# Six-layer decoder on one core: another agents' stage, alternating steps on VectorE, gates without diagonals, and new step sequences

## The chip, the core and the metric

The kernel runs on one NeuronCore of a Trainium2 chip. Its engines run their own instruction streams and meet through semaphores: TensorE (PE for matmuls, PEld for the loading of their stationary operand), VectorE (DVE), ScalarE (ACT), GpSimd (POOL) and SyncE (SP), which here issues all transfers. The metric is the device time of one execution in microseconds (us). The kernel before took 1081.24 us, the median of three runs from 1078.39 to 1082.4.

## The reference, cut to what matters

32 batches of 100 tokens, 256 features, fp32. Six layers follow each other, each ending in x = layernorm(x + layer(x)):

```
L0_attn : agent = x @ wq.w_conv1 ; key vector, softmax over 256, softmax over tokens, weighted sum of v -> one row per batch
L0_xattn: cross attention on ctx (361 keys) with a mask, 1 head
L0_ffn  : top 50 of 100 tokens by a sigmoid gate, 16-head attention among them
L1_attn : banded 16-head attention over all 100 tokens
L1_xattn: cross attention on ctx, 1 head
L1_ffn  : x/rms quantised to int8 steps (127/absmax, round, clip), times an int8 weight, times a scale
```

The first layer needs little per token: for each batch one 256-vector, scaled by a per-token factor `tok`, is added to x. All of its 32 vectors are computed ahead of everything else; that part is called the agents' stage here. Its steps: agent = x.w; y = the sum over tokens of agent times x; key row = y @ w_k0, softmaxed over 256 features; z = w_v0 times it; logits = z.x per token, softmaxed over tokens; u = the sum over tokens of that weight times x; the agent's vector v = u @ w_v0T.

## The kernel before, in words

**Streams and turns.** Two batches make a pair. Four streams A, B, C, D work on one pair each; a turn is one pair through all six layers, and each stream has four turns, 16 jobs in all. Each stream has its own SBUF tiles and two PSUM banks. Each engine's program for a stream is a Python generator whose `yield`s cut it into segments. `ORDER` holds one string per engine; `take` runs one segment of the named stream per letter, so the order on every engine is fixed, and an engine whose next segment waits does nothing else meanwhile. The strings come from a planner that is not part of the file.

**The agents' stage** (`tensor_agents`, `scalar_agents`, `vector_agents`, `gpsimd_agents`, and the transfers in `sync_first`) runs ahead of the turns on every engine. Eight slots of four batches are loaded. PE transposes x (L320), ACT copies the transposes out (L638), DVE computes `ag` (L804). When all transposes are done PE forms y as rows (L327: `ag` broadcast to 32 columns as the stationary operand, x moving, 256 columns). ACT and DVE copy the rows out of PSUM (`row`, L633 and L813), and `rows_to_columns` (L307) turns them into columns: 16 matmuls whose stationary operand is a 128x128 block. L336 is the key row, L307 is used again behind L392 (the rows u), L400 gives the vectors. The softmax over tokens is eight exponentials with sums on ACT (L647), a reciprocal and a division on DVE (L858), and L385, which turns the weights into columns. Products of weights for later layers (L299, L374, L380 and others, copied by `product`) lie between these steps on PE and DVE. The finished vectors go from SBUF to a DRAM tensor `agent_rows` (L1275), and `load_agent` (L1225) reads each pair's 2 KB row back, repeated over 100 partitions.

**Entry to the turns.** GpSimd clears the lower rows of `work` (L1111) and then `v_pick` and `v` of all streams (L1117, L1118), and goes on to its turns. DVE and ACT wait for the first of these (`agent_pool("rows")`), PE for `agent_dve("v")`; all wait for `ld_const`, every remaining weight.

**Masks.** `cell` and `seq` are single buffers for all streams. For each job GpSimd multiplies them (L1158), DVE makes two passes (L891, L893), ACT takes the logarithm (L665), GpSimd adds (L1162); only then does SP load the masks of the next stream in turn (`job`). In the first turn each stream's DVE program starts with its masks.

**Layernorm.** `stats` (L876) per batch: the residual `r`, then `bn_stats` (L878), then `bn_aggr` (L880), each waiting for the one before it; then the same for the second batch of the pair. GpSimd raises the variance to the power -1/2 (L1126), and `normalize` (L885) scales both batches.

**Gates.** DVE computes the gate of each token, multiplies the identity by it (L966, two diagonals), PE multiplies a matrix of ones by the diagonals (L473) so that each partition holds all gates, and DVE ranks them (L974, L977, batch after batch) and builds a selection matrix (L981). PE transposes that (L478) and gathers the chosen tokens (L482).

**Quantised layer** (L1076 to L1098): five small steps in a row, two scalings of 256 columns (L1085), rounding and clipping on 512 columns (L1088, L1090), then transposes and the product.

Of the kernel before, what the change touches and what calls it, by code (L numbers as in the profile page):

```python
# [50 lines left out]
class Steps:  # L51
# [8 lines left out]
    def up(self, name):  # L60
# [5 lines left out]
NORM = "r0 bn0 ag0 r1 bn1 ag1 x0 x1"  # L66
# [3 lines left out]
    "pick": "gates selT gath q k v hs0 hs tr0 tr1 av fo sc0 sc1",  # L70
# [7 lines left out]
    "pick": "ez selT xT q vs0 ex0 ex1 eT0 rT fo",  # L78
# [8 lines left out]
    "pick": "z0 z1 gp gt dg0 dg1 tie0 rk0 tie1 rk1 pk0 pk1 kT vs1 mx0 mx1 rd eT1 aT " + NORM,  # L87
    "local": "k0 k1 v1 " + " ".join(f"ma{i} mb{i} rd{i} eT{i} aT{i}" for i in range(NB * NC)) + " " + NORM,
    "second": "mx0 nb0 mx1 nb1 pT0 rs aT1 " + NORM,
    "quant": "am am2 am3 ra sc y0 y1 up yq os " + NORM,  # L90
}
GPSIMD = {
    "mask": "prod sum",
# [9 lines left out]
AGENT_TENSOR = ("w " + " ".join(f"x{n}" for n in range(16)) + " " + " ".join(f"y{n}" for n in range(8))  # L103
                + " yT1 key p0 p1 arT z p2 p3 log p4 p5 p6 col " + " ".join(f"u{n}" for n in range(8)) + " yT2 vec")
AGENT_SCALAR = " ".join(f"x{n}" for n in range(16)) + " row1 toke kexp lexp row2"
AGENT_VECTOR = ("w " + " ".join(f"ag{n}" for n in range(8)) + " tokd row1 tokr tok yT1 kmax p0 p1 krec kn aT zT p2 p3 lmax "
                "p4 p5 p6 lrec ln acol row2 w8 yT2 v")
# [10 lines left out]
def program(nc, ins, out):  # L118
    ctx = ExitStack()
    with ctx:  # L120
# [11 lines left out]
        qscale = sb("qscale", [P, 1])  # L132
# [18 lines left out]
        tok = sb("tok", [S, B])  # L151

# [3 lines left out]
        class Stream:  # L156
            def __init__(s, n):
# [22 lines left out]
                s.diag = s.eT[0:S, 0:T].rearrange("p (b t) -> p b t", b=NB)  # L180
                s.tie, s.above = s.eT[0:S, T:T + S], s.eT[0:S, T + S:T + 2 * S]
                s.pick = s.eT[0:S, T + 2 * S:T + 2 * S + NB * P].rearrange("p (b m) -> p b m", b=NB)
# [32 lines left out]
                s.ra = sb(f"ra{n}", [S, NB])  # L215
                s.os = sb(f"os{n}", [S, NB])
                s.load_x = Loaded(sem(f"load_x{n}"), 1)
                s.load_agent = Loaded(sem(f"load_agent{n}"), 1)
# [29 lines left out]
        y_rooms = [s.v[:, :, :, :].rearrange("p b h m -> p (b h m)")[:, 0:2 * D].rearrange("p (i d) -> p i d", i=2) for s in streams]  # L248
# [7 lines left out]
        b_room = SB_.kT[:, :, :, :].rearrange("p j c t -> p (j c t)")  # L256
        ag, tokd, toke, tokr, acol = (b_room[0:S, k * B:(k + 1) * B] for k in range(5))
        yT, aT_a, zT = (b_room[:, k * B:(k + NC) * B].rearrange("p (c b) -> p c b", c=NC) for k in (5, 7, 9))
        lstat = b_room[:, 11 * B:11 * B + 3 * SLOTS].rearrange("p (k i) -> p k i", k=3)
        a_room = SC_.kT[:, :, :, :].rearrange("p j c t -> p (j c t)")  # L260
        agent_w, arow, arow2 = a_room[:, 0:D], a_room[0:B, D:2 * D], a_room[0:B, 2 * D:3 * D]
        agent_v = SD.aT[0:B, :, :].rearrange("p c t -> p (c t)")[:, 0:D]
        astat = sb("astat", [B, 4])
# [9 lines left out]
        agent_rows = nc.dram_tensor("agent_rows", (NPAIR, NB * D), F32).ap()  # L273
        agent_kept = sem("agent_kept")
        ld_w0, ld_wk, ld_c, ld_const = (sem(n) for n in ("ld_w0", "ld_wk", "ld_c", "ld_const"))
# [4 lines left out]
        agent_pool = Steps(sem("agent_pool"), "rows zeros")  # L280
# [15 lines left out]
        def tensor_agents(e):  # L296
# [6 lines left out]
            def rows_to_columns():  # L303
                for c in range(NC):
                    for i in range(SLOTS):
                        at_ = (c * SLOTS + i) * ROWS
                        last = e.matmul(psum[:, 7, at_:at_ + ROWS], y_rooms[i // 2][:, i % 2, c * P:(c + 1) * P],  # L307
                                        ident[:, 0:P:32], start=True, stop=True)
                return last
# [13 lines left out]
            for i in range(SLOTS):  # L323
# [15 lines left out]
            e.wait_ge(ld_c, LD_C)  # L339
            spread(4, cols["a_bv"], W["a_o"]).then_inc(*agent_pe.up("p0"))  # L340
            spread(5, cols["c_bk"], W["c_qT"]).then_inc(*agent_pe.up("p1"))
# [10 lines left out]
            spread(4, cols["c_bv"], W["c_o"]).then_inc(*agent_pe.up("p2"))  # L352
            for c in range(NC):
                last = e.matmul(psum[:, 5, 0:1], cols["c_bk"][:, c:c + 1].to_broadcast([P, P]), cols["c_bq"][:, c:c + 1],
                                start=c == 0, stop=c == NC - 1)
            last.then_inc(*agent_pe.up("p3"))
# [9 lines left out]
            e.wait_ge(*agent_dve("p3"))  # L366
# [4 lines left out]
            last.then_inc(*agent_pe.up("p4"))  # L371
            for h in range(NC):
# [10 lines left out]
            e.wait_ge(*agent_dve("ln"))  # L383
            for i in range(SLOTS):
                last = e.matmul(psum[0:S, 7, i * ROWS:(i + 1) * ROWS], l_rooms[i // 4][:, i % 4, :], ident[:, 0:P:32],  # L385
                                start=True, stop=True)
            last.then_inc(*agent_pe.up("col"))
            e.wait_ge(*agent_dve("acol"))
            for i in range(SLOTS):
                for j in range(ROWS):  # L390
                    b = ROWS * i + j
                    last = e.matmul(psum[32 * j:32 * j + 32, i // 2, i % 2 * D:(i % 2 + 1) * D],  # L392
                                    acol[:, b:b + 1].to_broadcast([S, 32]), x_of(b), start=True, stop=True)
                last.then_inc(*agent_pe.up(f"u{i}"))
            e.wait_ge(*agent_act("row2"))
            e.wait_ge(*agent_dve("row2"))
            rows_to_columns().then_inc(*agent_pe.up("yT2"))
            e.wait_ge(*agent_dve("yT2"))
            for c in range(NC):
                last = e.matmul(psum[0:B, 6, 0:D], yT[:, c, :], W["w_v0T"][:, c, :], start=c == 0, stop=c == NC - 1)  # L400
            last.then_inc(*agent_pe.up("vec"))
            e.wait_ge(*agent_dve("v"))
            e.wait_ge(ld_const, LD_CONST)
# [249 lines left out]
        def scalar_turns(e, s):  # L653
# [42 lines left out]
            for t in range(TURNS):  # L696
# [20 lines left out]
                if t == 0:  # L717
                    e.wait_ge(*agent_pool("zeros"))
# [749 lines left out]
```

## Time and profile before

| what | value |
|---|---|
| median of 3 runs | 1081.24 us |
| the profiled execution, its own time | 1081.67 us |
| span of its profile | 1079.9 us |
| PE busy | 900.4 us, 83% |
| DVE busy | 704.7 us, 65% |
| ACT busy | 514.2 us, 48% |
| POOL busy | 371.4 us, 34% |
| mean granted TensorE clock | 0.876 |

Times in the profile count from the start of the span. Busy time is the time in which an engine has at least one instruction; a granted clock of 1.00 is TensorE's 2.4 GHz and 0.50 is 1.2 GHz. The profiled execution ran 0.43 us above the median.

### The profile page before, as it was taken

How to read it: one execution, taken by the hardware profiler on the slowest of the kernel's cores; microseconds unless marked ns; L12 is line 12 of the kernel's file. 1: busy time of each engine (PE TensorE's matmuls, PEld its weight loads, DVE VectorE, ACT ScalarE, POOL GpSimd, SP SyncE). 2: the span in 40 equal slices, each digit the busy share in tenths (PEclk: the TensorE clock that was granted, in tenths of full speed). 3: DMA queues.
4: the chain of work that ended last, by engine and by line, in shares of the span. 5: the costliest groups of instructions: out<-in, count | busy, mean ns of one | idle time of the engine just before them, and what ended most of it. 6: DMA issues, size and time to landing. Idle time of an engine off the chain costs nothing.

```text
span 1079.9 us, 19738 instructions
## 1 busy us (share of the span) xinstructions
PE 900.4 (83%) x7022; PEld 671.0 (62%) x7022; DVE 704.7 (65%) x2081; ACT 514.2 (48%) x2392; POOL 371.4 (34%) x528
## 2 busy tenths in 40 slices
PE   7957798898798699998889788897979688997983
PEld 5735677565577587665567566574647466765662
DVE  4235666565777857567697876558487686766576
ACT  3102244766542345865433355664535144556641
POOL 0045401344463322254443422236144232223243
PEclk9766898999888799997889699898869898998896
DMA  7801400002214000002032200011030400000000
GB/s 227 285 32 44 157 1 2 2 8 85 92 55 144 24 1 2 2 23 73 30 123 75 78 9 2 12 69 34 11 102 1 144 17 1 1 2 1 1 1 31
DMA packets 23382, 54.10 MB, mean 50 GB/s; under 512 B 3696, under 2 KB 9588, under 8 KB 23284
## 3 DMA queue, kind: packets, MB, share of 16 engines
q1 hardware_dynamic: 23284, 52.84, 14.7%
q8 instruction: 55, 0.90, 0.3%
q14 instruction: 43, 0.35, 0.1%
HBM read 49.53 MB, written 3.31 MB: 49 GB/s over the span
## 4 chain that ended last, share of the span: by engine, by line
PE 50%; DVE 26%; ACT 10%; POOL 5%; issue 4%; DMA 4%; SPq 1%; DVEq 0%; POOLq 0%; ACTq 0%
PE psum L419 8%; PE psum L424 8%; PE psum L458 7%; ACT work L763 4%; PE psum L444 4%; DVE bn L878 4%; PE psum L578 4%; PE psum L589 3%; ACT work L728 3%; DVE x L885 3%; PE psum L599 2%; DVE mx L1040 2%; PE psum L581 2%; DVE res L945 1%; DVE mv L880 1%
## 5 line engine op out<-in xcount | busy, mean ns | idle before, releaser
L763 ACT ACTIVATE work<-psum,mx 100x100 f32<-100x100 f32 x512 | 169.8, 369 | 53.1 <-DVE mx L1040 52.8
L1124 POOL TENSOR_SCALAR ve<-mv 100x2 f32<-100x2 f32 x96 | 21.7, 226 | 289.7 <-DVE mv L880 289.4
L763 ACT ACTIVATION_READ_ACCUMULATOR work<-psum,mx 100x1 f32 x512 | 118.5, 232 | 0.0
L657 ACT ACTIVATE xT<-psum 128x100 f32<-128x100 f32 (+3 forms) x144 | 53.0, 374 | 124.5 <-PE psum L594 55.9
L458 PE MATMUL psum<-eT,ctx 128*128 128x100 f32 x768 | 103.6, 292 | 7.0 <-DVE eT L914 6.7
L458 PEld LDWEIGHTS psum<-eT,ctx 128*128 128x128 f32 x768 | 99.6, 207 | 10.5 <-DVE eT L914 8.9
L1153 POOL COPY work<-rden 100x128 f32<-100x128 f32 (+1 forms) x80 | 25.1, 314 | 201.4 <-DVE rden L1044 172.6
L444 PE MATMUL psum<-ctxT,qT 128*100 128x361 f32 x256 | 92.6, 508 | 2.1 <-ACT qT L657 1.2
L657 ACT ACTIVATE eT<-psum 100x400 f32<-100x400 f32 (+3 forms) x128 | 64.1, 513 | 49.1 <-PE psum L617 21.2
L878 DVE BATCH_NORM_STATS2 bn<-res 100x6 f32<-100x256 f32 x192 | 82.1, 427 | 6.6
L1040 DVE TENSOR_REDUCE mx<-psum 100x4 f32<-100x400 f32 x128 | 66.9, 565 | 26.4 <-PE psum L581 26.2
L589 PE MATMUL psum<-ident,work 100*100 100x100 f32 x512 | 71.8, 273 | 14.1 <-ACT work L763 13.8
L885 DVE TENSOR_SCALAR x<-res,mv,rstd 100x256 f32<-100x256 f32 x160 | 73.5, 504 | 13.4 <-POOL rstd L1126 13.0
L728 ACT ACTIVATE work<-psum,mx 128x50 f32<-128x50 f32 x256 | 73.8, 349 | 16.4 <-DVE mx L999 16.3
L589 PEld LDWEIGHTS psum<-ident,work 100*100 100x100 f32 x512 | 54.5, 140 | 30.3 <-ACT work L763 22.8
L1126 POOL TENSOR_TENSOR rstd<-ve,minus_half 100x2 f32<-100x2 f32 x96 | 69.3, 722 | 8.0
L578 PE MATMUL psum<-kT,qT 64*100 64x400 f32 x256 | 64.5, 583 | 6.7 <-DVE aT L1051 6.6
L444 PEld LDWEIGHTS psum<-ctxT,qT 128*100 128x100 f32 x256 | 44.4, 181 | 36.0 <-issue 8.0
L1146 POOL TENSOR_TENSOR kT<-work,heads 128x400 f32<-128x400 f32 x64 | 54.4, 853 | 32.9 <-DVE work L1029 32.9
L728 ACT ACTIVATION_READ_ACCUMULATOR work<-psum,mx 128x1 f32 x256 | 63.3, 253 | 0.0
L1046 DVE COPY eT<-psum 100x400 f32<-100x400 f32 x64 | 35.5, 554 | 38.1 <-PE psum L589 37.8
L414 PE MATMUL psum<-ident,x 100*128 100x100 f32 x192 | 31.9, 294 | 28.7 <-DVE x L885 28.6
(231 smaller groups left out, 2066.3 us busy)
## 6 DMA issues: line engine op xcount, KB each, us to landing
ctx<-in_ctx SPq DMA_DIRECT2D x16, 768.0 KB, 7.0
ctxT<-in_ctxT SPq DMA_DIRECT2D x16, 722.0 KB, 4.3
cell<-in_cell SPq DMA_DIRECT2D x16, 282.0 KB
seq<-in_seq SPq DMA_DIRECT2D x16, 282.0 KB
x<-in_x SPq DMA_DIRECT2D x16, 200.0 KB
eT<-agent_rows SPq DMA_DIRECT2D x16, 200.0 KB
out<-xplus SPq DMA_DIRECT2D x16, 200.0 KB
work<-in_x SPq DMA_DIRECT2D x4, 400.0 KB
```

The lines of the kernel that those rows point to most:

```text
L419: last = e.matmul(dst, w[:, c, h * P:(h + 1) * P], n(c), start=c == 0, stop=c == NC - 1)
L424: last = e.matmul(dst, xT(c), w[:, c, :], start=c == 0, stop=c == NC - 1)
L444: last = e.matmul(bk[b][0:S, 0:S2], s.qT[:, c, b * S:(b + 1) * S], s.ctxT[:, b, c, :], start=c == 0, stop=c == NC - 1)
L458: last = e.matmul(bk[b][:, c * S:(c + 1) * S], s.ctx[:, b, j, c * P:(c + 1) * P], s.pT[:, b, j, :], start=j == 0, stop=j == S2C - 1)
L578: e.matmul(bk[g][0:S, 0:4 * S], s.qT[r:r + 64, c, b * S:(b + 1) * S], s.keys[r:r + 64, i % 2, :, :], start=True, stop=False, skip_group_ch ...
L589: last = e.transpose(bk[g][0:S, q * S:(q + 1) * S], s.e[:, 4 * g + q, :], ident[0:S, 0:S])
L657: return e.activation(dst, src, ACT.Copy, **kw)
L728: last = e.activation(s.e_pick[:, 4 * g + i, j, 0:CAP], bk[g][:, at_:at_ + CAP], ACT.Exp, bias=s.mx[:, h:h + 1], accum_out=s.den[:, h:h + 1])
L763: last = e.activation(s.e[:, h, :], bk[g][0:S, q * S:(q + 1) * S], ACT.Exp, bias=s.mx[0:S, h:h + 1], accum_out=s.den[0:S, h:h + 1])
L878: e.bn_stats(s.bn[:, b, :], s.res[0:S, b, :]).then_inc(*dve.up(f"bn{b}"))
L885: e.tensor_scalar(dst[0:S, b, :], s.res[0:S, b, :], s.mv[:, b, 0:1], s.rstd[:, b:b + 1], ALU.subtract, ALU.mult).then_inc(*dve.up(f"x{b}"))
L1040: e.tensor_reduce(s.mx[0:S, 4 * g:4 * g + 4], bk[g][0:S, 0:4 * S].rearrange("p (h k) -> p h k", k=S), AX, ALU.max, negate=True).then_inc(* ...
```

## The change

**Agents' stage.** y is formed as columns at once: per batch and half of the features one matmul with x (100x128) as the stationary operand and one column of `ag` moving. Each slot's eight such matmuls stand behind the transposes of the next slot. The softmax over tokens subtracts the maximum on DVE (two instructions), takes two exponentials without sums, and is not divided; its sum comes from one matmul with ones and scales the finished vector. The vectors stay in SBUF (`agent_v`, 32 partitions); each is copied from its one partition to the 100 partitions of a stream's tile by a transfer of its own. The weight products p1, p3, p4, p5, p6 stand later on PE.

**Masks and transfers.** In the first turn each stream has its own room for the masks. All four are loaded early and go through the agents' programs of POOL, DVE and ACT; the turns start with the mix. PE and the others wait for the first few weights (`ld_first`) at the entry and for the rest at the first pick. `zeros` moves into the turns of POOL.

**Turns.** The steps of both batches alternate (r0 r1 bn0 bn1 ag0 ag1), as do those of the ranking; the diagonals go; the gather precedes the transposes of the selection; the quantised layer loses two small steps and rounds batch by batch. All five sequences in `ORDER` are new (PE 816 letters as before, DVE 748 for 752, ACT 716 for 720, POOL 364 for 368, SP 52 for 58); their letters are left out here.

```diff
-NORM = "r0 bn0 ag0 r1 bn1 ag1 x0 x1"
+NORM = "r0 r1 bn0 bn1 ag0 ag1 x0 x1"
# tensor_agents
+            def weighed(i, weights):
+                for j in range(ROWS):
+                    b = ROWS * i + j
+                    for c in range(NC):
+                        last = e.matmul(psum[:, 7, c * B + b:c * B + b + 1], x_of(b)[:, c * P:(c + 1) * P],
+                                        weights[:, b:b + 1], start=True, stop=True)
+                return last
...
-            for i in range(SLOTS):
-                e.wait_ge(*agent_dve(f"ag{i}"))
-                for j in range(ROWS):
-                    b = ROWS * i + j
-                    last = e.matmul(psum[32 * j:32 * j + 32, i // 2, i % 2 * D:(i % 2 + 1) * D],
-                                    ag[:, b:b + 1].to_broadcast([S, 32]), x_of(b), start=True, stop=True)
-                last.then_inc(*agent_pe.up(f"y{i}"))
-            e.wait_ge(*agent_act("row1"))
-            e.wait_ge(*agent_dve("row1"))
-            rows_to_columns().then_inc(*agent_pe.up("yT1"))
+                if i:
+                    e.wait_ge(*agent_dve(f"ag{i - 1}"))
+                    weighed(i - 1, ag).then_inc(*agent_pe.up(f"y{i - 1}"))
+            e.wait_ge(*agent_dve("ag7"))
+            weighed(SLOTS - 1, ag).then_inc(*agent_pe.up("y7"))
...
# vector_agents, behind the logits
+            for k in range(2):
+                e.tensor_tensor(l_rooms[k], psum[:, k, :].rearrange("p (i t) -> p i t", t=P)[:, :, 0:S],
+                                lstat[:, 4 * k:4 * k + 4].unsqueeze(2).to_broadcast([P, SLOTS // 2, S]), ALU.add).then_inc(
+                    *agent_dve.up(f"sub{k}"))
...
+            for s in streams[2:4]:
+                masks_clip(e, s, 0)
+            e.wait_ge(*agent_pe("vec"))
+            e.tensor_scalar(agent_v[:, :], psum[0:B, 6, 0:D], astat[:, 3:4], None, ALU.mult).then_inc(*agent_dve.up("v"))
...
# gpsimd_agents
+            for s in streams:
+                masks_product(e, s, 0)
+            for s in streams:
+                masks_sum(e, s, 0)
+            e.wait_ge(*SD.gpsimd["mask"]("sum", 0))
             e.wait_ge(*agent_pe("u7"))
             for s in streams:
                 last = e.memset(s.work[32 * (ROWS - 1):P, 0:H * HALF], 0.0)
             last.then_inc(*agent_pool.up("rows"))
...
# vector_turns
-            def stats(dve, t, b):
-                e.wait_ge(*dve(f"r{b}", t))
-                e.bn_stats(s.bn[:, b, :], s.res[0:S, b, :]).then_inc(*dve.up(f"bn{b}"))
-                e.wait_ge(*dve(f"bn{b}", t))
-                e.bn_aggr(s.mv[:, b, :], s.bn[:, b, :]).then_inc(*dve.up(f"ag{b}"))
+            def stats(dve, t):
+                for b in range(NB):
+                    e.wait_ge(*dve(f"r{b}", t))
+                    e.bn_stats(s.bn[:, b, :], s.res[0:S, b, :]).then_inc(*dve.up(f"bn{b}"))
+                for b in range(NB):
+                    e.wait_ge(*dve(f"bn{b}", t))
+                    e.bn_aggr(s.mv[:, b, :], s.bn[:, b, :]).then_inc(*dve.up(f"ag{b}"))
...
# load_agent, and the place of it in sync_first
         def load_agent(e, s, t):
-            e.dma_start(s.agent.rearrange("p b d -> p (b d)"),
-                        agent_rows[s.pair(t):s.pair(t) + 1, :].to_broadcast([S, NB * D])).then_inc(s.load_agent.sem, 16)
+            for b in range(NB):
+                n = NB * s.pair(t) + b
+                e.dma_start(s.agent[:, b, :], agent_v[n:n + 1, :].unsqueeze(1).to_broadcast([1, S, D])).then_inc(s.load_agent.sem, 16)
...
             e.wait_ge(*agent_dve("v"))
-            e.dma_start(agent_rows.rearrange("n (b d) -> (n b) d", b=NB), agent_v).then_inc(agent_kept, 16)
-            e.wait_ge(agent_kept, 16)
             for s in streams:
                 load_agent(e, s, 0)
+            for s in (SC_, SD):
+                load_ctx(e, s, 0)
```

DVE's new sequence begins `BADCABDCABAC`: the mixes of B, A, D and C stand ahead of the first `normalize`, which is A's. `weighed` multiplies in fp32, as all matmuls here do except the quantised layer's and the band's.

## Rows read from the trace of the kernel before

**Rows 1.** The page's busy time of each engine, and the chain of waits by engine.
```profile
PE 900.4 (83%) x7022; PEld 671.0 (62%) x7022; DVE 704.7 (65%) x2081; ACT 514.2 (48%) x2392; POOL 371.4 (34%) x528
PE 50%; DVE 26%; ACT 10%; POOL 5%; issue 4%; DMA 4%; SPq 1%; DVEq 0%; POOLq 0%; ACTq 0%
```

**Rows 2.** Windows: stretch, length, busy time and instructions per engine, clock, DMA share, GB/s.
```profile
83.00:160.00 77.00, 64.37 (x430) 51.55 (x430) 45.95 (x144) 25.70 (x96) 26.34 (x27) 0.83 0.20 70
160.00:1000.00 840.00, 720.79 (x5734) 535.71 (x5738) 576.92 (x1680) 439.94 (x2110) 303.64 (x436) 0.89 0.12 39
1000.00:1080.00 80.00, 56.75 (x404) 39.79 (x396) 53.78 (x152) 32.62 (x146) 27.20 (x45) 0.82 0.03 11
```

**Rows 3.** Timeline of PE to the first turn: start, length, line, tiles, forms, count.
```profile
4.80 2.07 PE L299 MATMUL psum<-res,w_conv_c 128*128 128x256 f32 x4 [4.80 <-DMA ident<-in_ident]
20.71 1.59 PE L320 MATMUL psum<-ident,ctxT 100*128 100x100 f32 x8 [1.10 <-DMA ctxT<-in_x]
29.41 5.54 PE L307 MATMUL psum<-ident,v 128*128 128x4 f32 x32 [0.92 <-DVE v L813]
43.38 1.11 PE L299 MATMUL psum<-xplus,c_bv_c 128*128 128x256 f32 x4
48.97 0.34 PE L362 MATMUL psum<-aT,kT 128*32 128x100 f32 x8
55.84 1.58 PE L385 MATMUL psum<-ident,qT 128*100 128x4 f32 x16 [1.99 <-DVE qT L858]
57.70 3.14 PE L392 MATMUL psum<-work,kT 100*32 100x256 f32 x32 [0.28 <-DVE kT L862]
70.19 1.92 PE L400 MATMUL psum<-xplus,kT 128*32 128x256 f32 x4 [0.32 <-DVE kT L869]
83.06 0.90 PE L414 MATMUL psum<-ident,x 100*128 100x100 f32 x4 [10.96 <-DVE x L885]
```

**Rows 4.** Windows of line L307 on PE alone: stretch, length, busy, clock, DMA.
```profile
29.00:31.00 2.00, 1.59 (x15) 0.99 1.10 308
31.00:35.00 4.00, 3.95 (x19) 0.50 1.06 353
```

**Rows 5.** Timeline of DVE: the agents' stage, and the first mixes.
```profile
7.72 0.42 DVE L804 SCALAR_TENSOR_TENSOR x<-work,kT 100x256 f32<-100x256 f32 x1
8.07 0.42 DVE L804 SCALAR_TENSOR_TENSOR x<-work,kT 100x256 f32<-100x256 f32 x1
72.15 0.41 DVE L871 COPY aT<-psum 32x256 f32<-32x256 f32 x1 [2.01 <-PE psum L400]
78.40 0.48 DVE L945 SCALAR_TENSOR_TENSOR res<-eT,tok,x 100x256 f32<-100x256 f32 x1
78.91 0.43 DVE L878 BATCH_NORM_STATS2 bn<-res 100x6 f32<-100x256 f32 x1
79.47 0.45 DVE L945 SCALAR_TENSOR_TENSOR res<-eT,tok,x 100x256 f32<-100x256 f32 x1
80.42 0.18 DVE L880 BATCH_NORM_AGGREGATE mv<-bn 100x2 f32<-100x6 f32 x1
119.56 0.45 DVE L966 TENSOR_SCALAR eT<-ident,gate 100x100 f32<-100x100 f32 x2
120.95 0.48 DVE L945 SCALAR_TENSOR_TENSOR res<-eT,tok,x 100x256 f32<-100x256 f32 x1
```

**Rows 6.** Timeline of POOL: the clearing of four tiles, and one mask sum.
```profile
63.14 3.90 POOL L1111 MEMSET work<- 32x1024 f32 x4 [62.70 <-PE psum L392]
79.49 2.01 POOL L1162 TENSOR_TENSOR kT<-cell,kT 100x722 f32<-100x722 f32 x1 [2.22 <-ACT cell L665]
```

**Rows 7.** Two windows of all engines, as in rows 2, and one transfer issue.
```profile
75.00:79.00 4.00, 0.00 (x0) 0.00 (x0) 1.55 (x4) 0.40 (x1) 2.23 (x2) 0.50 0.57 194
261.00:263.00 2.00, 2.00 (x10) 1.56 (x11) 1.93 (x6) 1.94 (x13) 0.16 (x1) 1.00 1.02 406
agent_rows<-aT SPq DMA_DIRECT2D x1, 32.0 KB, 1.4
```

More of the change, by code:

```diff
@@ L351, in tensor_agents @@
             last.then_inc(*agent_pe.up("z"))
[L352 to L356, printed above, removed]
+            spread(5, cols["c_bv"], W["c_o"]).then_inc(*agent_pe.up("p2"))
             e.wait_ge(*agent_dve("zT"))
@@ L371, in tensor_agents @@
             last.then_inc(*agent_pe.up("p4"))
+            e.wait_ge(*agent_act("row2"))
+            e.wait_ge(*agent_dve("row2"))
+            for c in range(NC):
+                for i in range(SLOTS):
+                    at_ = (c * SLOTS + i) * ROWS
+                    last = e.matmul(psum[:, 7, at_:at_ + ROWS], u_rooms[i // 2][:, i % 2, c * P:(c + 1) * P],
+                                    ident[:, 0:P:32], start=True, stop=True)
+            last.then_inc(*agent_pe.up("yT2"))
+            e.wait_ge(*agent_dve("yT2"))
+            for c in range(NC):
+                last = e.matmul(psum[0:B, 6, 0:D], yT[:, c, :], W["w_v0T"][:, c, :], start=c == 0, stop=c == NC - 1)
+            last.then_inc(*agent_pe.up("vec"))
+            e.wait_ge(*agent_dve("p3"))
             for h in range(NC):
@@ L382, in tensor_agents @@
             last.then_inc(*agent_pe.up("p6"))
[L383 to L403, printed above, removed]
+            e.wait_ge(ld_first, LD_FIRST)
         def tensor_turns(e, s):
@@ L623, in tensor_turns, with masks_log @@
                 yield
+        def masks_log(e, s, t):
+            part = mask_rooms(s, t)[0]
+            e.wait_ge(*s.vector["mask"]("clip", t))
+            e.activation(part, part, ACT.Ln).then_inc(*s.scalar["mask"].up("ln"))
         def scalar_agents(e):
             e.preload_act_table_set("natural_log_exp_and_others")
-            def row(name, first, last_, scale):
-                for k, after in ((0, first), (1, last_)):
-                    e.wait_ge(*agent_pe(after))
-                    last = e.activation(y_rooms[k].rearrange("p i d -> p (i d)"), psum[:, k, :], ACT.Copy, scale=scale)
-                last.then_inc(*agent_act.up(name))
             for n in range(NC * SLOTS):
@@ L773, in scalar_turns @@
                 if t + 1 < TURNS:
-                    masks(t + 1)
+                    masks_log(e, s, t + 1)
                     yield
@@ new lines, in vector_agents @@
+            product(wqbk[:, :], 4, 1)
+            product(bqbk[:, :], 5, 3)
+            e.wait_ge(*agent_pe("col"))
+            e.tensor_copy(acol, psum[0:S, 7, 0:B]).then_inc(*agent_dve.up("acol"))
+            e.wait_ge(*agent_pe("sum"))
+            e.reciprocal(astat[:, 3:4], psum[0:B, 6, D:D + 1]).then_inc(*agent_dve.up("rsum"))
+            for k, ready in ((2, "u5"), (3, "u7")):
+                e.wait_ge(*agent_pe(ready))
+                last = e.tensor_copy(u_rooms[k][:, :, :].rearrange("p i d -> p (i d)"), psum[:, k, :])
@@ L1103, in vector_turns, with masks_product, masks_sum @@
                 yield
-        def gpsimd_agents(e):
+        def masks_product(e, s, t):
+            part, other = mask_rooms(s, t)
+            e.wait_ge(*s.load_mask(t))
+            e.tensor_tensor(part, part, other, ALU.mult).then_inc(*s.gpsimd["mask"].up("prod"))
+        def masks_sum(e, s, t):
+            e.wait_ge(*s.scalar["mask"]("ln", t))
+            e.tensor_tensor(s.lm[:, :, :], mask_rooms(s, t)[0], s.lm[:, :, :], ALU.add).then_inc(*s.gpsimd["mask"].up("sum"))
+        def gpsimd_agents(e):
+            for s in streams:
+                masks_product(e, s, 0)
+            for s in streams:
+                masks_sum(e, s, 0)
+            e.wait_ge(*SD.gpsimd["mask"]("sum", 0))
             e.wait_ge(*agent_pe("u7"))
@@ L1112, in gpsimd_agents @@
             last.then_inc(*agent_pool.up("rows"))
[L1113 to L1119 removed]
+            e.wait_ge(ld_first, LD_FIRST)
         def gpsimd_turns(e, s):
```

419 lines of the change are left out of this document (202 added, 217 removed).

## The prediction

> **What bounds the kernel now.** I read the busy times first, then the chain, then windows from end to end, then the agents' stage and the first mixes on each timeline. PE is busy 83% of the span, yet half of the chain of waits runs over other engines, DVE with 26% ahead of them [rows 1]. So neither PE's work alone nor one engine's latency sets the time; four streams keep PE filled up to a point. I measure PE's work as busy time times granted clock. In the long middle it is 720.79 x 0.89 / 840 = 0.764 us per us [rows 2]. From 83 to 160 us 64.37 x 0.83 = 53.4 us get done, which the middle's pace would do in 69.9 us; the ramp therefore loses 7.1 us. That is less than its look suggests (the fourth stream's mix is at 120.95 us [rows 5], 42.6 us behind the first), because two or three streams nearly fill PE. The first 83 us hold no turn at all: PE's first transposes for a turn are at 83.06 [rows 3].
>
> **The clock at the start.** The records give no lower clock before 31 us, but the matmuls do: the four of L299 take 2.07 us at 4.80 and 1.11 us at 43.38 [rows 3]. So the first stretch runs at 1.2 GHz, transposes and all. L307 shows the two levels in one block: 15 records in 1.59 us at 0.99, 19 in 3.95 us at 0.50 [rows 4], or 0.11 and 0.21 us a record, with two records to a matmul, and that while PE was busy without a gap.
>
> **Part 1, y as columns.** Out go L327, the row copies and the first L307, which ends at 29.41 + 5.54 = 34.95 us [rows 3]. In come 64 matmuls, 128 records, that load a stationary operand as wide as L307's for one moving column; no row shows this form, and L307's 0.21 us is the nearest. The stage then is one block on PE: it starts at 6.87 (L299's end), eight slots of transposes at 1.59 make 12.7 us, 128 x 0.21 make 26.9, and the end is at 46.5 us, 11.5 later than now. At the other level it would be 14.1 us for the sums and 33.7 us for the end, 1.3 earlier; both are kept as ends. I take the slow one: neither the transposes, at 80% of PE's time, nor L307, at all of it, held or won the full clock in this trace, and the new block is nothing but these two kinds. The arrival of x (the last slot at 20.71) no longer matters.
>
> **Part 2, from there to the vectors.** Now 34.95 to 72.56 (L871's end [rows 5]) is 37.6 us. The logits end at 49.31 and their columns start at 55.84 [rows 3]; in between are a maximum, eight exponentials, a reciprocal and a division. The new order has a maximum, two additions and two exponentials half beside each other: 3.0 us for 6.5, a gain of 3.5. One weight product of 2 us (L299's form) leaves the way ahead of the transposed key row: gain 2. Moved in are p4 between u and its columns (1 us) and the sum's matmul (0.3). Mask passes of C and D now stand in front of the vectors' copy on DVE; PE's 1.92 us of L400 [rows 3] covers most of them, and I add 0.1. Gain 4.1; bounds 0 and 7. The vectors are ready at 46.5 + 33.5 = 80.0 us for 72.56.
>
> **Part 3, the copies of the vectors.** Eight transfers of 100 KB each read one SBUF partition a hundred times. Nothing like it is in the trace. Today's four transfers from DRAM move 800 KB inside the 4 us window from 75 us [rows 7]: the low end, all eight there 5 us behind the vectors. The only transfer that reads this tile takes 1.4 us for its 32 KB [rows 7], 23 GB/s: the high end, 35 us. Between them lies the pace of a single queue engine: 406 GB/s on 16 of them [rows 7] is 25.4 each. If one partition gives its bytes to one engine's worth of traffic at a time, a copy takes 102.4 KB / 25.4 = 4.0 us and eight take 32. I take this, nearest to the row that reads the same tile.
>
> The Trainium skill, "SBUF — State Buffer", section "Door 1: The DMA port swizzle", speaks against the change here too: a transfer's bandwidth depends on how many of 16 ports its partitions reach, and one partition reaches one. With its 436 GB/s over 16 ports a copy would be 3.8 us and the eight 30 us (an estimate from the page); the forecast would be 2 us lower. No row here reads from one partition.
>
> The wait is placed badly. DVE's sequence has the mixes of B, A, D and C ahead of the first normalisation, so all four streams stand behind the last copy. D's mix starts at 80.0 + 1 for the latency + 32 = 113. DVE then has two mixes of 1.73 (below), POOL's root meanwhile, and a normalisation of 0.7: PE's first transposes come at 117.2 for 83.06, 34.1 later. What would stand there if the copies were fast is POOL: at the vectors two mask sums of 2.01 and the clearing of 3.90 [rows 6] are left, so DVE may enter at 88; four mixes and a normalisation give 95.7 on PE, 12.6 later than now.
>
> **Part 4, the ramp.** All masks are done, so four streams start together. I let the new ramp lose 3 us (some 4 to 6 us at half clock) for 7.1: gain 4.1, bounds 0 and 7.
>
> **Part 5, the turns.** A mix of two batches takes 80.42 + 0.18 - 78.40 = 2.20 us [rows 5]: a step that waits for the one before starts 0.51 us behind it (78.40 to 78.91), an independent one 0.35 (7.72 to 8.07). Alternating, r0 r1 bn0 bn1 ag0 ag1 end at 1.73, a gain of 0.47. It counts fully in mix, pick, local and quant, 64 times, 30 us; in the two cross stages the first batch's steps now wait for the second's result, and I count 0.2 for 32 of them, 6 us. The diagonals are 0.45 us each pair [rows 5], 16 times, 7 us; ranking, quantising and the gather ahead of the transposes together 1 us a job, 16 us. PE's share of the gates stays as it is (two 100-column matmuls for one of 200). Sum 59 us of steps, not all on the path: DVE has 26% of a 1079.9 us chain for 704.7 busy, 0.40 [rows 1], so 24 us by that. Since a shortened step often uncovers another wait I take 14; bounds 0 and 24. The sequences themselves are worth plus or minus 8.
>
> The Trainium skill, "VectorE: DVE Perf Modes", section "The DRAIN you can't avoid", says that waits between VectorE's instructions cost nothing and only their number counts. By that rule alternation is worth nothing. The 0.51 and 0.35 above disagree with it, so I give it a small chance below.
>
> Later turns also load their vectors this way, 24 copies of 4.0 us instead of 12 transfers. They are issued well ahead, but x of the next turn queues behind them: cost 4, bounds 0 and 20.
>
> **Sum.** 34.1 - 4.1 - 14 + 4 = +20.0 us on the profiled execution's own 1081.67 (span 1079.9 and 1.8 around it; 0.43 above the median): 1101.7, said as 1102 us. Chance 0.45, its own range 1088 to 1116.
>
> **Rivals.**
> - A, cheap copies: the eight vectors arrive within 5 us, and POOL's chain sets the start. 12.6 - 4.1 - 14 = -5.5: 1076 us, the side of faster. For it: four such transfers take 4 us today; against it: these read DRAM, not one partition. It decides wherever the eight copies need under about 10 us, since POOL covers that much. Chance 0.27.
> - B, full clock in the first block: y ends at 33.7, 12.8 earlier: 1089 us. For it: PE would be without gaps; against: so it was in L307. Chance 0.11.
> - A and B together: vectors at 67, POOL lets DVE in at 75, PE starts at 83: 1081.67 - 0.3 - 4.1 - 14 = 1063 us. Chance 0.09.
> - C, alternation saves nothing: 9 of the 14 us stay: 1111 us. Chance 0.08.
>
> **How the numbers follow.** About 0.5%, 5.4 us, is what a measurement of this kernel can tell from no change, so same is 1075.8 to 1086.7. A straddles its lower edge, half of it faster; A with B is faster; the forecast, B and C are mostly slower. Faster 0.12 + 0.09 + 0.08 from the low ends of the forecast and B (a larger part 5) = 0.29; same 0.13 from A and 0.05 from the edges of B and the forecast = 0.18; slower 0.53. The range takes in A with a few us below it and C with a few above, and leaves out most of A with B: 1066 to 1116.
>
> **What would show it.** Part 1: on PE's timeline the one-column matmuls at 0.21 us a record and the last near 46 us; under 36 us it was B. Part 3: the idle time of DVE's first `res` behind a transfer, the mix of D at 110 us or later; under 95 us it was A, and then POOL's clearing must end just before. Part 4: PE's windows behind its first turn should reach 0.76 at once. Part 5: starts of r0 and r1 0.35 apart, `bn` 0.35 apart, and a middle stretch whose pace is 1 to 2% above 0.764. If the middle is slower than now, the new sequences cost more than the steps give, which nothing in this trace can tell, and the sum is wrong there.

## The result, and the profile after

The changed kernel takes 1087.53 us, the median of 20 runs (1078.17 to 1097.23), beside 1081.01 us for the kernel before on the same chip: a ratio of 1.0058, with a 95% interval of 1.0037 to 1.0079. It is slower by 6.5 us. The forecast was 1102 us, 20 slower: the direction held and the range held it, the size did not. The profiled execution of the changed kernel took 1083.32 us, 4 below its median. The medians further down are of 4 to 10 executions; one of e4_ports's ten took 1626 us, and without it that median would be 1076.8 for 1077.2.

Page of the changed kernel, busy times and chain of waits, beside [rows 1]:
```profile
PE 888.7 (82%) x7088; PEld 678.3 (63%) x7088; DVE 660.4 (61%) x2062; ACT 511.2 (47%) x2376; POOL 377.4 (35%) x528
PE 54%; DVE 20%; ACT 10%; DMA 5%; SPq 4%; issue 3%; POOL 3%; DVEq 0%; POOLq 0%
```
DVE lost 44 us of work and a quarter of its share of the chain; DMA and SP's queue took 4 points more between them. Windows, as in [rows 2]:
```profile
83.00:160.00 77.00, 43.10 (x250) 35.30 (x251) 37.87 (x128) 15.13 (x51) 24.00 (x32) 0.77 0.26 56
160.00:1000.00 840.00, 717.71 (x5946) 541.63 (x5944) 541.10 (x1678) 447.78 (x2153) 307.24 (x437) 0.91 0.14 39
1000.00:1080.00 80.00, 59.08 (x402) 41.47 (x398) 53.79 (x156) 32.78 (x145) 28.09 (x44) 0.82 0.03 10
110.00:160.00 50.00, 42.82 (x250) 34.98 (x249) 30.30 (x102) 15.13 (x51) 21.43 (x27) 0.91 0.08 31
```
The first stretch does 43.10 x 0.77 = 33 us of work for 53 before, since no turn runs in it before 109.71. The middle runs at 717.71 x 0.91 / 840 = 0.778 for 0.764, and what is left over at the end is much the same. Once the turns have started, the pace is that of the middle at once: 42.82 x 0.91 / 50 = 0.779. PE's timeline, beside [rows 3]:
```profile
20.41 3.46 PE L311 MATMUL psum<-qT,work 100*128 100x1 f32 x16
39.16 6.87 PE L311 MATMUL psum<-qT,ctxT 100*128 100x1 f32 x32
48.19 2.08 PE L302 MATMUL psum<-a_o,a_bv_c 128*128 128x256 f32 x4
51.81 1.11 PE L302 MATMUL psum<-xplus,c_bv_c 128*128 128x256 f32 x4
109.71 1.57 PE L422 MATMUL psum<-ident,x 100*128 100x100 f32 x8 [32.60 <-DVE x L902]
```
The one-column matmuls take 3.46 / 16 = 0.216 us a record (0.21 forecast), and the block ends at 46.03; 46.5 was forecast. PE's first transposes for a turn come at 109.71 (83.06 before, 117.2 forecast): 26.7 us later than before, where the forecast had 34.1. Its 32.60 us of idle time end on DVE. DVE's timeline, and below it SP's:
```profile
74.30 0.47 DVE L883 TENSOR_SCALAR agent_v<-psum,vs 32x256 f32<-32x256 f32 x1
92.13 0.88 DVE L954 SCALAR_TENSOR_TENSOR res<-eT,tok,x 100x256 f32<-100x256 f32 x2 [14.28 <-DMA eT<-agent_v]
92.92 0.75 DVE L894 BATCH_NORM_STATS2 bn<-res 100x6 f32<-100x256 f32 x2
93.59 0.30 DVE L897 BATCH_NORM_AGGREGATE mv<-bn 100x2 f32<-100x6 f32 x2
93.81 0.86 DVE L954 SCALAR_TENSOR_TENSOR res<-eT,tok,x 100x256 f32<-100x256 f32 x2
105.85 0.88 DVE L954 SCALAR_TENSOR_TENSOR res<-eT,tok,x 100x256 f32<-100x256 f32 x2 [10.30 <-DMA eT<-agent_v]
```
```profile
74.80 22.79 SPq L1242 DMA_DIRECT2D eT<-agent_v  x8
```
The vectors are ready at 74.77 (80.0 forecast), B's mix stands behind the fourth copy at 92.13, D's behind the eighth at 105.85: 31.1 us for eight copies, 3.9 each, the forecast's 32 + 1. A mix of two batches takes 93.59 + 0.30 - 92.13 = 1.76 us from its first start to its last end (1.73 forecast), for 2.20 in [rows 5]. SP's queue itself is held 22.79 us over issuing the eight.

### The profile page after: what moved, and what is told of

Read it like the earlier page. It is cut to its first block, busy times and chain, and to the rows that moved or that the text cites. A ratio compares the mean times of both kernels' runs of the same rounds, so it can differ in the third digit from the quotient of the medians.

```text
span 1081.5 us, 19882 instructions
## 1 busy us (share of the span) xinstructions
PE 888.7 (82%) x7088; PEld 678.3 (63%) x7088; DVE 660.4 (61%) x2062; ACT 511.2 (47%) x2376; POOL 377.4 (35%) x528
## 4 chain that ended last, share of the span: by engine, by line
PE 54%; DVE 20%; ACT 10%; DMA 5%; SPq 4%; issue 3%; POOL 3%; DVEq 0%; POOLq 0%
PE psum L427 9%; PE psum L466 8%; PE psum L432 7%; ACT work L736 4%; PE psum L452 4%; ACT work L771 4%; PE psum L592 4%; PE psum L603 3%; DVE x L902 3%; DVE bn L894 3%; PE psum L311 2%; SPq L1242 2%; PE psum L613 2%; DMA x<-in_x 2%; DMA seq<-in_seq 2%
## 5 line engine op out<-in xcount | busy, mean ns | idle before, releaser
L771 ACT ACTIVATION_READ_ACCUMULATOR work<-psum,mx 100x1 f32 x512 | 122.5, 241 | 0.0
L902 DVE TENSOR_SCALAR x<-res,mv,rstd 100x256 f32<-100x256 f32 x160 | 78.7, 538 | 12.6 <-POOL rstd L1142 12.3
L452 PE MATMUL psum<-ctxT,qT 128*100 128x361 f32 x256 | 83.7, 470 | 1.6 <-ACT qT L687 1.4
L1142 POOL TENSOR_TENSOR rstd<-ve,minus_half 100x2 f32<-100x2 f32 x96 | 71.9, 749 | 8.0
L422 PE MATMUL psum<-ident,x 100*128 100x100 f32 x192 | 32.7, 292 | 51.0 <-DVE x L902 50.7
L894 DVE BATCH_NORM_STATS2 bn<-res 100x6 f32<-100x256 f32 x192 | 71.2, 412 | 0.0
L1162 POOL TENSOR_TENSOR kT<-work,heads 128x400 f32<-128x400 f32 x64 | 54.4, 860 | 28.1 <-DVE work L1035 28.1
L422 PEld LDWEIGHTS psum<-ident,x 100*128 100x128 f32 x192 | 22.9, 160 | 61.4 <-issue 34.2
```

Source lines behind the costliest of these rows:

```text
L452: last = e.matmul(bk[b][0:S, 0:S2], s.qT[:, c, b * S:(b + 1) * S], s.ctxT[:, b, c, :], start=c == 0, stop=c == NC - 1)
L771: last = e.activation(s.e[:, h, :], bk[g][0:S, q * S:(q + 1) * S], ACT.Exp, bias=s.mx[0:S, h:h + 1], accum_out=s.den[0:S, h:h + 1])
L894: e.bn_stats(s.bn[:, b, :], s.res[0:S, b, :]).then_inc(*dve.up(f"bn{b}"))
L902: e.tensor_scalar(dst[0:S, b, :], s.res[0:S, b, :], s.mv[:, b, 0:1], s.rstd[:, b:b + 1], ALU.subtract, ALU.mult).then_inc(*dve.up(f"x{b}"))
L1142: e.tensor_tensor(s.rstd[:, :], s.vare[:, :], minus_half[0:S, 0:NB], ALU.pow).then_inc(*pool.up("rstd"))
```

## The experiments

All times are medians; the kernel before had 1081.0 to 1082.8 us beside them, and each ratio is to it.

**1. Vectors through DRAM (e1_dram).**
```
+ e.dma_start(agent_rows..., agent_v[:, :]).then_inc(agent_kept, 16)
+ e.wait_ge(agent_kept, 16)
- for b in range(NB): e.dma_start(s.agent[:, b, :], agent_v[n:n + 1, :]...to_broadcast([1, S, D]))
+ e.dma_start(s.agent, agent_rows[pair:pair + 1, :].to_broadcast([S, NB * D]))
```


> The changed kernel, except that the agents' vectors go to the first mixes through DRAM as in the kernel before: one store of 8 rows, one wait, then one load of 200 KB per stream, instead of eight copies of 100 KB from one partition each. Theory S (the forecast's third part: the eight copies are what holds the start): the vectors are ready at 74.8 us as before the edit, the loads land some 6 us later (72.15 to 78.40 in the kernel before), VectorE enters the turns at 81.4 behind the zeroing on GpSimd, four mixes of 1.7 us, TensorE's first transposes at 88 to 89 us (109.7 now), the total 21 us shorter than the changed kernel: about 1067. Rival H (the copies only hide other work that is as late: masks, memsets, context loads): the first transposes stay behind 100 us and the total stays within 8 us of 1087.5. Rival M (the earlier start is given back, because the first turns then compete with the loads of the contexts C and D): the transposes start at 88 but the stretch up to 200 us loses over 8 us of it, total 1075 or more.

Measured: 1046.66 us, ratio 0.9665 (0.961 to 0.972). That is 41 us under the changed kernel, where theory S had 21. DVE and PE:
```profile
70.42 0.47 DVE L885 TENSOR_SCALAR agent_v<-psum,vs 32x256 f32<-32x256 f32 x1
77.57 0.88 DVE L956 SCALAR_TENSOR_TENSOR res<-eT,tok,x 100x256 f32<-100x256 f32 x2 [3.66 <-POOL work L1135]
84.75 1.56 PE L424 MATMUL psum<-ident,x 100*128 100x100 f32 x8 [11.57 <-DVE x L904]
```
From the vectors to the first transposes it is 84.75 - 70.89 = 13.9 us, for 109.71 - 74.77 = 34.9: 21 us, as S had it (the vectors themselves were ready 3.9 us earlier, of which more in the last section). The other 16 to 20 us came later in the kernel. DVE's waits in the changed kernel, in total, times and longest, show a candidate:
```profile
DVE res L954 <- DMA eT<-agent_v: 24.6, 2, 14.3
DVE res L954 <- DMA x<-in_x: 18.8, 2, 13.9
```
In the kernel before the second is 6.7 us in all, in the DRAM kernel 7.9. SP's and DVE's timeline of the changed kernel at that place:
```profile
863.91 1.53 SPq L1242 DMA_DIRECT2D eT<-agent_v  x2
865.55 0.43 SPq L1237 DMA_DIRECT2D x<-in_x  x1
875.47 0.88 DVE L954 SCALAR_TENSOR_TENSOR res<-eT,tok,x 100x256 f32<-100x256 f32 x2 [13.94 <-DMA x<-in_x]
```
The load of x goes out right behind a pair of copies (another pair went out at 855.13) and lands 10 us later.

**2. Only the later turns copy from one partition (e9_later_copies).**
```
+ source = agent_v[n:n + 1, :]...to_broadcast([1, S, D]) if t else agent_rows[n // NB, b * D:(b + 1) * D]...
```


> The changed kernel with the eight vectors of the first turn loaded from DRAM (100 KB each) and the 24 of the later turns copied from one partition each, as in the changed kernel. The kernel with all of them from DRAM took 1046.7 us, 41 less than the changed kernel, and its start was only 25 us earlier. Theory L (the later copies hold up what the same queue issues behind them: in the changed kernel VectorE waited 4.8 and 13.9 us for two loads of x issued right behind such copies): start at 85 us as with DRAM, the two waits for x back, total 1062 to 1067. Rival F (later copies cost nothing; the other 16 us came from the context loads C and D being issued late in the first turn, 97.6 to 104.9 us, or from another interleaving): total within 4 us of 1046.7, no wait for x over 5 us.

Measured: 1059.38 us (0.9759 to 0.985 as a ratio). It is theory L's case, a little under its 1062 to 1067: the later copies cost 12.7 us. Start and wait are as it says:
```profile
89.75 1.56 PE L424 MATMUL psum<-ident,x 100*128 100x100 f32 x8 [10.40 <-DVE x L904]
DVE res L956 <- DMA x<-in_x: 19.0, 2, 13.9
```
The waits for x have 11 us more than in the DRAM kernel (19.0 for 7.9), the total 12.7. So the eight first copies cost 1087.5 - 1059.4 = 28.1 us by the medians, 21.7 by the profiled spans (1081.5 and 1059.8). By the way from the vectors to PE's first transposes it is 21.1 (34.9 for 89.75 - 75.89 = 13.9).

**3. The copies in another order (e4_ports).**
```
+ for n in (0, 4, 1, 5, 2, 6, 3, 7): e.dma_start(streams[n // NB].agent[:, n % NB, :], agent_v[n:n + 1, :]...)
```


> The changed kernel with the same eight copies in another order: streams A and C in turn, then B and D, so that two copies that follow one another read partitions four apart (0, 4, 1, 5, ...). Theory Q (the copies of one queue are served one behind the other, each bound by its one partition, 3.9 us): the last one lands as late as now, near 105.5 us, and TensorE starts within 1 us of 109.7 (the stream whose turn is first may wait longer, at most 8 us more at the start). Rival P (neighbouring partitions share a path and could overlap if they were apart): the eight land in 16 to 20 us, near 93, and TensorE starts near 98, total about 1076.

Measured: 1077.19 us, ratio 0.9929 (0.9894 to 0.9965). Q falls, P holds:
```profile
78.15 14.06 SPq L1298 DMA_DIRECT2D eT<-agent_v  x8
95.39 0.88 DVE L954 SCALAR_TENSOR_TENSOR res<-eT,tok,x 100x256 f32<-100x256 f32 x2 [13.08 <-DMA eT<-agent_v]
102.05 1.35 DVE L902 TENSOR_SCALAR x<-res,mv,rstd 100x256 f32<-100x256 f32 x4
```
The vectors were ready at 78.12, DVE waited once, until 95.39, and then ran its four mixes without a gap: the eight land in 17.3 us for 31. The transfers' own pace says the same (windows of the changed kernel, then of this one; the last number is GB/s):
```profile
84.00:88.00 4.00, 0.00 (x0) 0.00 (x0) 0.00 (x0) 0.00 (x0) 0.00 (x0) 0.50 0.47 27
```
```profile
84.00:88.00 4.00, 0.00 (x0) 0.00 (x0) 0.00 (x0) 0.00 (x0) 0.69 (x1) 0.70 0.49 56
```

**4. The control for it (e11_tiles).** The same edit with (0, 2, 1, 3, 4, 6, 5, 7).

> The changed kernel with the eight copies in the order of partitions 0, 2, 1, 3, 4, 6, 5, 7: neighbours in the queue go to different streams' tiles, as in the run with the order 0, 4, 1, 5, ..., but read partitions of the same four. That run landed all eight in 17 us (31 in the changed kernel). Theory G (copies from partitions of the same group of four can't overlap, copies from different groups do): the first four serial, then the next four, first mixes behind D's copy at 30 to 31 us after the vectors, total as the changed kernel, 1085 to 1088. Rival W (what can't overlap is two copies into one tile): all landed 17 us behind the vectors, first transposes near 103, total near 1077.

Measured: 1083.85 us (1.0 to 1.0048). Vectors at 76.43, the last group's mix at 107.50, 31.1 us behind them:
```profile
107.50 0.88 DVE L954 SCALAR_TENSOR_TENSOR res<-eT,tok,x 100x256 f32<-100x256 f32 x2 [10.32 <-DMA eT<-agent_v]
```
The copies alternate between two tiles but stay within four partitions, and they don't overlap: it is the source partitions that count (theory G).

**5. The sums as rows (e2_yrows), 6. and with DRAM (e3_both).**
```
- weighed(i, ag)                      # 64 one-column matmuls into psum 7
+ matmul(psum rows, ag[:, b]...to_broadcast([S, 32]), x_of(b))   # 32, then two row copies each on ACT and DVE
+ rows_to_columns()                   # 16 matmuls of 4 columns
```


> The changed kernel, except that the weighted sums over the tokens are built as in the kernel before: as rows in PSUM, copied by ScalarE and VectorE, and turned into columns by 16 matmuls; the eight copies from one partition stay. Theory C (the 128 one-column matmuls cost 11.5 us at the start): the block ends near 35 us (46.0 now), the vectors are ready near 63.7 us if the stretch behind it keeps its 28.7 us, near 69 if TensorE's clock in it is the half one as in the kernel before; eight copies of 3.9 us behind them, the first transposes at 98.6 to 104, the total 1076 to 1082. Rival (the block is hidden, what follows waits for the weights' or x's loads): the vectors stay at 73 to 75 us, the total within 2 us of 1087.5.

> The changed kernel with both edits: sums as rows, vectors through DRAM. If the two prices stand behind one another (the forecast's way of adding them): vectors at 63.7 to 69 us, VectorE in the turns at 70.5 to 76, TensorE's first transposes at 78 to 83, the total 1056 to 1061, faster than both kernels. If the zeroing and the mask sums on GpSimd are the bound once both are gone: VectorE enters the turns at 81 whatever the vectors do, first transposes at 88, total 1067 as with the DRAM edit alone. If the turns' part of the change gives back what the start gains: about 1075 or more.

Measured: 1074.08 us (0.9917 to 0.9968), 13.4 under the changed kernel; and 1039.14 us (0.9528 to 0.9655), 7.5 under the DRAM kernel. PE and DVE with rows and copies (e2):
```profile
34.72 0.99 PE L311 MATMUL psum<-ident,a_v 128*128 128x4 f32 x4
68.43 0.47 DVE L895 TENSOR_SCALAR agent_v<-psum,vs 32x256 f32<-32x256 f32 x1
103.96 1.56 PE L427 MATMUL psum<-ident,x 100*128 100x100 f32 x8 [30.27 <-DVE x L914]
```
The block ends at 35.7 us for 46.0, so the columns cost 10.3 us on PE. From there to the vectors it is 33.2 us, for 28.7 in the changed kernel, and in the other two kernels with rows 32.4 and 32.0, for 28.6 to 32.7 in the other kernels with columns and the masks in the agents' stage (mean of these eight 30.1). So some 2 us of the 10 come back behind the columns, on average, and the single execution varies by more. The two prices stand behind one another: the rows take 13.4 us off the changed kernel, 7.5 off the DRAM kernel, and 7.9 in the pair of experiments 10 and 12.

**7. Alternation undone (e5_serial), 8. and done alone (e7_before_alt).**
```
- NORM = "r0 r1 bn0 bn1 ag0 ag1 x0 x1"     (e7: + in the kernel before, - in e5)
+ NORM = "r0 bn0 ag0 r1 bn1 ag1 x0 x1"
```


> The kernel with the vectors through DRAM (1046.7 us) and the residual steps of both batches one behind the other again, as before the change (r0 bn0 ag0 r1 bn1 ag1); everything else, the sequences too, stays. Theory A (the forecast's price: the alternation saves 9 us): 1056. Theory A2 (of the 45 us that the turns lost against the kernel before, alternation is the greater part, since these steps stand in the chain of waits): 1065 to 1075. Rival C (alternation saves nothing, the steps lie beside other work): within 3 us of 1046.7.

> The kernel before with one edit: the residual steps of both batches in turn (r0 r1 bn0 bn1 ag0 ag1), everything else as before, its sequences too. The reverse edit in a later kernel cost 20.5 us. Theory A2 (the alternation is worth 20 us by itself, since these steps stand in the chain of waits wherever they are): 1058 to 1063. Theory A (9 us, as forecast): 1070 to 1073. Rival I (the 20 us came from the fit between alternation and the rest of the change): 1076 to 1081.

Measured: 1067.17 us (0.9834 to 0.9963), 20.5 above its base; and 1061.19 us, ratio 0.9809 (0.9749 to 0.987), 19.8 under the kernel before. A2 both times. The mixes of e5:
```profile
81.92 0.48 DVE L954 SCALAR_TENSOR_TENSOR res<-eT,tok,x 100x256 f32<-100x256 f32 x1 [1.33 <-POOL work L1133]
83.00 0.45 DVE L954 SCALAR_TENSOR_TENSOR res<-eT,tok,x 100x256 f32<-100x256 f32 x1
84.05 0.47 DVE L954 SCALAR_TENSOR_TENSOR res<-eT,tok,x 100x256 f32<-100x256 f32 x1
```
From one pair's start to the next it is 84.05 - 81.92 = 2.13 us, for 1.68 in the changed kernel (92.13 to 93.81). Over the kernel DVE's busy time differs by 685.3 - 659.0 = 26.3 us in the first comparison and 704.7 - 673.2 = 31.5 in the second: 78 and 63% of it come out of the total.

**9. Diagonals and the longer quantised layer back (e12_long_quant).**
```
+ for b in range(NB): e.tensor_scalar(s.diag[:, b, :], ident[0:S, 0:S], s.gate[:, b:b + 1], None, ALU.mult)
+ e.tensor_scalar(s.sc, s.ra, 127.0, ...); "up" and "yq" over both batches at once
```


> The kernel with the vectors through DRAM (1046.7 us) and, as in the kernel before, the diagonals for the gates (two steps on VectorE, one matmul of ones with them) and the longer quantised layer (four single-column steps, rounding steps over both batches at once); alternation and sequences stay as changed. Theory 1 (5 us, as forecast): 1050 to 1054. Theory 2 (worth as much above the forecast as the alternation was, 2.3 times): 1056 to 1060. Rival (these steps lie beside other work): within 2 us of 1046.7.

Measured: 1055.04 us (0.9693 to 0.979), 8.4 above its base, between the two theories. DVE's busy time is 17.8 us more (676.8 for 659.0): 47% of it counts. With the 26.3 of the alternation these are 44.1 of the 44.3 us that DVE lost. The other steps of part 5, the ranking and the gather ahead of the transposes, were not tried by themselves.

**10. The sequences of the kernel before (e6_old_order).**
```
- "DVE": ("BADCABDCABACABABDBDCB...
+ "DVE": ("AABAABAACABABCABABADC...        # likewise PE, ACT, POOL, SP
```


> The kernel with the vectors through DRAM (1046.7 us) and the step sequences of the kernel before, fitted to the new numbers of steps (the mask steps of the first turn dropped, the zeroing step put in). Theory O (the sequences are worth 8 us at most either way, as forecast): 1039 to 1055. Theory O2 (the new sequences carry most of the 45 us that the turns gained): 1065 to 1085.

Measured: 1042.77 us (0.9606 to 0.9681), 3.9 under its base: the new sequences seem to cost a little. Four executions on each side (1038 to 1045 and 1038 to 1051) hardly bear such a difference; experiments 6 and 12 have 4.2 the same way. PE:
```profile
85.61 0.90 PE L424 MATMUL psum<-ident,x 100*128 100x100 f32 x4 [6.75 <-DVE x L904]
```
That is 10.2 us behind the vectors (75.38) for 13.9: the old order has A's mix and normalisation ahead of C's and D's mixes.

**11. The first turn's masks back in the turn (e13_masks_in_turns).**
```
+ if t == 0: masks_clip(e, s, 0); yield        # likewise product, log and sum; out of the agents' stage
```


> The kernel with the vectors through DRAM and the sequences of the kernel before (1042.8 us), with the first turn's mask steps (product, clip, logarithm, sum) moved from the agents' stage back into the first turn, as steps of the streams, as in the kernel before; the masks' tiles and their early loads stay. Theory 4 (the forecast: their place in the turn cost the ramp 4 us): 1045 to 1049. Theory R (what the other runs leave over of the difference between the kernels, 8 to 14 us, is this): 1051 to 1057. Rival N (beside other work in either place, and GpSimd's zeroing comes earlier without them): 1039 to 1044.

Measured: 1046.21 us (0.9623 to 0.9736), 3.4 above its base. It agrees with theory 4, but 3.4 us is no more than medians of four runs (1038 to 1045 and 1042 to 1053) can bear.

**12. The best of them (e10_best): DRAM, rows, old sequences.**

> The changed kernel with three edits: vectors through DRAM, sums as rows, and the step sequences of the kernel before. Alone, the first gave 1046.7, with the second 1039.1; the third took 3.9 us off the first. If they add: 1035 us, some 46 under the kernel before. If the old sequences only suited the start with the sums as columns: 1039 or above.

Measured: 1034.90 us, ratio 0.9564 (0.9518 to 0.9609): 46 us under the kernel before and 53 under the changed one. They add. Windows, as in [rows 2]:
```profile
83.00:160.00 77.00, 68.38 (x582) 55.73 (x581) 49.01 (x181) 30.29 (x131) 22.46 (x32) 0.94 0.00 1
160.00:1000.00 840.00, 735.97 (x5943) 547.60 (x5942) 557.92 (x1708) 459.22 (x2199) 318.95 (x456) 0.91 0.12 39
```
The middle's pace is 0.797 for 0.764, and 0.778 in the changed kernel. How finely this measure tells kernels apart shows in e9_later_copies, whose middle has the changed kernel's code:
```profile
160.00:1000.00 840.00, 715.07 (x5824) 536.28 (x5821) 542.62 (x1665) 445.81 (x2143) 312.40 (x446) 0.90 0.14 39
```
It gives 0.766, and the clock is rounded to 0.01. So 0.797 is clear of 0.764, while the forecast's sign of 1 to 2% can't be read off one execution.

## Why the forecast was right in direction and wrong in size

| step | forecast | measured |
|---|---|---|
| part 1, columns | +11.5 | +8.6 at the vectors; totals +7.5, +7.9, +13.4 |
| part 2, to the vectors | -4.1 | -6.0 |
| part 3, vectors to PE's first transposes | +26.7 | +24.4 on the forecast's own measure; totals +28.1 (spans +21.7) |
| part 4, masks ahead | -4.1 | -3.4 |
| part 5, alternation | -9 | -19.8, -20.5 |
| part 5, the other steps | -5 | -8.4 |
| part 5, sequences | 0 (8 either way) | +3.9 |
| later turns' copies | +4 | +12.7 |

The step that failed is part 5: it was priced at 14 us and measures 28.6, and the alternation in it at 9 (so rival C has it) and measures 20. The step beside it that failed is the later copies' price, 4 us for 12.7, which hides more than half of that. A third part of the miss lies in the start: PE's first transposes are 26.7 us later than before, not 34.1.

- **Part 1** was right on PE (46.03 for 46.5). Over nine kernels with columns the vectors are ready between 70.9 and 78.1 us, 75.2 on average; over the three with rows at 68.9, 65.2 and 65.6, 66.6 on average. The difference is 8.6. Part 2's measured figure is 66.6 less the 72.56 of the kernel before.
- **Part 2** fits with rows, 32.0 to 33.2 us for the forecast's 33.5. With columns it is 28.7 in the changed kernel and 30.1 on average. The forecast subtracted from the way of the kernel before, and there half of the logits ran at half speed (0.89 us for 16 records, 0.52 for the last); in the changed kernel's trace all of them, from 52.85 us on, take 0.53 to 0.55.
- **Part 3** was right in mechanism and nearly in size: one partition, 3.9 us a copy, all four streams behind the last. The forecast's 26.7 is its 34.1 less parts 1 and 2; on the same measure the way from the vectors to PE's first transposes grew from 83.06 - 72.56 = 10.5 us to 34.9, by 24.4. Some 3.4 of this belong to the new sequences (13.9 for 10.5 us with DRAM), which the forecast counted here too.
- **Part 4** holds by its sign: from 110 to 160 us PE has the middle's pace at once. Moving the masks alone gave no more than the noise.

The Trainium skill, "SBUF — State Buffer", section "Door 1: The DMA port swizzle", goes further than the forecast used it: its table puts partitions 0 to 3 on one of the 16 ports and 4 to 7 on another. The runs agree with it for these eight partitions: copies in the order 0, 4, 1, 5 overlap (17.3 us for eight), copies in the order 0, 2, 1, 3 do not (31.1 us).

- **Part 5.** The forecast counted 59 us of shortened DVE steps, where the busy times show 26.3 to 31.5 for the alternation and 17.8 for the rest, took DVE's share of the chain (0.40 of its busy time) for 24 us, and then cut this to 14 because a shortened step often uncovers another wait. The runs give 20.2 + 8.4 = 28.6 us. The residual steps are worth 0.63 to 0.78 of their DVE time, well over the engine's average share of 0.40; the diagonals and the quantised layer, at 0.47, lie near it. Two things were wrong, then: the cut from 24 to 14, which no row called for, and the engine's mean share as the measure for the residual steps. The trace before could have told part of it:
```profile
L878 DVE BATCH_NORM_STATS2 bn<-res 100x6 f32<-100x256 f32 x192 | 82.1, 427 | 6.6
```
That line holds 3.9% of the chain of waits, 42 us for 82.1 busy, a share of 0.51. Why a saved microsecond there counts for even more was argued and not measured: in the code each such step stands between two matmul groups of its own stream, with nothing of that stream beside it.
- **The later copies** failed the other way: foreseen (x queues behind them), priced at 4 of a range to 20, measured 12.7. In the changed kernel both errors stand in one middle stretch and cancel in good part, so its pace of 0.778 looks like the forecast's own 1 to 2%; only the DRAM runs pulled them apart. That the total came within 15 us of the forecast is in part luck: with part 5 alone put right the forecast would have been near 1087, with the later copies alone near 1110.
- **Rivals.** A and A with B needed quick copies and are out by 31.1 us; B's full clock in the first block did not come (0.216 us); C is out by the alternation's 20 us.

The Trainium skill, "VectorE: DVE Perf Modes", section "The DRAIN you can't avoid", measured eight copies with a semaphore behind each and with one behind the last, and found that the semaphore costs nothing extra. That doesn't carry over to a step that waits for the one right before it: here the same instructions with the same semaphores, in another order, gave 19.8 and 20.5 us.

**What stays open.** The measured terms, with 20.2 for the alternation, sum to +15.3 us and the kernel shows +6.5; with the spans' 21.7 in part 3 the sum is +8.9. The rest is within what medians of four to ten runs leave, or the terms don't quite add: most were measured on the DRAM kernel, with its earlier start. No run tells which of the two it is.

## What to carry to other kernels

Don't spread many rows out of one group of SBUF partitions, least of all on the queue that also carries the next inputs: with a store and four broadcast loads through DRAM, DVE had its first mix 6.7 us behind the vectors, and even then it was GpSimd's clearing that it waited for; this saved 41 us. Price a shortened step by its own line's share of the chain of waits and by where it stands in its stream, not by its engine's mean share; two dependent chains of short steps on one engine are to be interleaved. And when a change of many parts lands near its forecast, measure the parts before believing the working.

## What the runs showed of the hardware

- Two copies from one group of partitions, 0 to 3 or 4 to 7, run one behind the other at 102.4 KB in 3.9 us (26 GB/s; 27 in the window at 84 us), also when they fill different tiles; from different groups they overlap, 2.2 us each (56 GB/s). Groups beyond the first eight partitions were not tried alone.
- A queue of such copies blocks its issuer as well: SP took 22.79 us for issuing eight, and the context loads of C and D behind them went out from 97.6 us on.
- The clock in the records of the first 50 us can't be taken at its word where it says 1.00. Windows of the DRAM kernel and of the changed one, the same code at this place:
```profile
32.00:38.00 6.00, 6.00 (x32) 6.00 (x31) 0.00 (x0) 1.12 (x3) 3.42 (x2) 0.50 0.73 241
```
```profile
32.00:38.00 6.00, 6.00 (x32) 6.00 (x33) 0.00 (x0) 1.01 (x2) 1.71 (x1) 1.00 0.67 209
```
One says 0.50 and the other 1.00, yet both ran their one-column matmuls at 3.46 us for 16 records, and the changed kernel's L302 took 2.08 us at 48.19 and 1.11 at 51.81 with 1.00 in both places. The DRAM kernel shows this form at both levels; its windows give 1.00 from 6 to 10 us, 0.72 to 15 and 0.50 from there:
```profile
9.65 1.87 PE L313 MATMUL psum<-qT,work 100*128 100x1 f32 x16
16.68 3.46 PE L313 MATMUL psum<-qT,work 100*128 100x1 f32 x16
```
So 3.46 us is the level of 1.2 GHz, and rival B's price for the other, 0.11 us a record, was right (1.87 / 16 = 0.117). In these traces the durations tell the level, not the column.
- When the full clock comes differs from one execution to the next, and with it the start: nearly the same code had its vectors ready anywhere from 70.9 to 78.1 us. The earliest of these had the full level for three blocks at 9 to 12 us, as above; in the latest, e4_ports, L302 still took 2.05 us at 52.06.
